# Tokens and output weights turned by transposing DMAs instead of matmuls in a BitNet attention plus quantised MLP layer

## What is computed

```
xn  = (x - mean) / sqrt(var + 1e-5)                      # per token
q, k, v = bitnet(xn, wq), bitnet(xn, wk), bitnet(xn, wv)  # 1024, 256, 256 channels
bitnet(x, w) = nan_to_num((x @ sign(w).T) * mean|w| * scale)
att = softmax(q k^T / sqrt(32)) v       # 32 heads of 32, 8 heads of keys and values
out = x + bitnet(att, wo) + (silu(xn @ G) * (xn @ U)) @ D   # G, U, D int4-like, dequantised, 3584 wide
```

## Time and profile before

| | |
|---|---|
| median of three runs | 2337.19 us |
| span of the profiled execution, first to last instruction | 2335.8 us |
| difference of the two, taken as what lies around the span | 1.4 us |
| PE busy | 2284.4 us, 98% of the span |
| DVE, ACT, POOL busy | 1809.7, 1591.0, 990.0 us |
| projections (chunks 0 to 3, `project`) | about 27 to 237 us |
| output groups (`attend_output`) | 1032.7 to 1148.6 us |

### The profile page before, as it was taken

One profiled execution on the slowest core, in us unless ns is written; L12 is line 12 of the kernel. 1 busy time (PEld: TensorE's weight loads), 2 busy tenths in 40 slices (PEclk: granted clock), 3 DMA queues, 4 the chain that ended last, 5 costly groups with the idle time before them and its releaser, 6 DMA issues.

```text
span 2335.8 us, 44834 instructions
## 1 busy us (share of the span) xinstructions
PE 2284.4 (98%) x18443; PEld 1100.0 (47%) x18443; DVE 1809.7 (77%) x2313; ACT 1591.0 (68%) x2051; POOL 990.0 (42%) x559
## 2 busy tenths in 40 slices
PE   6999999999999999999999999999999999999998
PEld 3444455555555555534444444444444444444444
DVE  8878888888888888856677777777777777777777
ACT  6774788888888888872366666666665666666664
POOL 0450699999999999960022222210002222221000
PEclk9999999999999999999999999999999999999999
DMA  5891344444444444443111111121114111114111
GB/s 187 171 202 32 70 72 78 74 76 70 72 81 72 74 72 73 80 92 136 59 37 36 44 47 37 36 109 45 37 64 145 36 36 37 38 53 181 36 36 72
DMA packets 178305, 175.51 MB, mean 75 GB/s; under 512 B 87778, under 2 KB 127586, under 8 KB 178102
## 3 DMA queue, kind: packets, MB, share of 16 engines
q1 hardware_dynamic: 113590, 143.28, 19.5%
q0 software_dynamic: 64512, 29.37, 12.6%
HBM read 160.08 MB, written 65.45 MB: 97 GB/s over the span
## 4 chain that ended last, share of the span: by engine, by line
PE 90%; DVE 5%; ACT 2%; issue 1%; DMA 1%; SPq 0%; POOL 0%; DVEq 0%; ACTq 0%
PE ps L1676 33%; PE ps L1692 17%; PE ps L1448 9%; PE ps L1501 9%; PE ps L1515 9%; PE ps L1647 5%; PE ps L1530 4%; PE ps L1473 3%; DVE sm L977 1%; DVE zone L1112 1%; DVE zone L1016 1%; ACT zone L809 0%; ACT zone L741 0%; ACT zone L789 0%; DVE zone L1388 0%
## 5 line engine op out<-in xcount | busy, mean ns | idle before, releaser
L1676 PE MATMUL ps<-xT,zone 128*128 128x512 f16 x3584 | 774.6, 379 | 2.7 <-DVE zone L1388 2.7
L1131 DVE TENSOR_REDUCE zone<-ps 128x1 f32<-128x512 f32 x1024 | 639.1, 683 | 128.1 <-PE ps L1448 120.0
L809 ACT ACTIVATE zone<-ps,sm 128x512 f32<-128x512 f32 x1024 | 628.8, 693 | 115.3 <-PE ps L1501 110.9
L649 POOL TENSOR_TENSOR zone<-zone 128x1024 f32<-128x1024 f32 x252 | 619.1, 2543 | 123.9 <-ACT zone L809 70.0
L1365 DVE TENSOR_SCALAR ps<-ps,zone_c 128x1024 f32<-128x1024 f32 x392 | 506.7, 1293 | 160.5 <-PE ps L1676 158.5
L932 ACT ACTIVATE ps<-ps,zone_c 128x1024 f32<-128x1024 f32 x392 | 426.7, 1088 | 259.9 <-PE ps L1676 259.9
L1676 PEld LDWEIGHTS ps<-xT,zone 128*128 128x128 f16 x3584 | 350.3, 98 | 426.2 <-DVE zone L1388 4.2
L1448 PE MATMUL ps<-zone 96*32 96x512 f16 (+1 forms) x3946 | 437.3, 380 | 8.6 <-issue 3.6
L1501 PE MATMUL ps<-zone 98*32 98x512 f16 x4096 | 438.3, 381 | 4.5 <-ACT zone L809 4.2
L1692 PE MATMUL ps<-zone 128*128 128x512 f16 x1792 | 387.1, 379 | 0.0
L684 POOL CAST zone<-zone 128x1024 f16<-128x1024 f32 x56 | 58.1, 1037 | 692.2 <-DVE zone L1369 692.2
(11 more groups left out here) (138 smaller groups left out, 1387.6 us busy)
## 6 DMA issues: line engine op xcount, KB each, us to landing
zone<-dequantised SPq DMA_DIRECT2D x84, 512.0 KB, 3.6
dequantised<-zero_points SPq DMA_DIRECT2D x56, 256.0 KB, 4.0
zone<-zone SPq DMA_DIRECT2D x384, 32.0 KB, 2.3
zone<-_attn_hidden_states_dram SPq DMA_DIRECT2D x16, 512.0 KB, 6.6
zone<-inverse_sums SPq DMA_DIRECT2D x128, 64.0 KB, 2.0
attention<-zone SPq DMA_DIRECT2D x32, 256.0 KB, 2.0
xT<-attention SPq DMA_DIRECT2D x4, 2048.0 KB, 12.2
dequantised<-zero_points POOLq DMA_DIRECT2D x28, 256.0 KB, 11.2
```

What stands on the lines that cost most here:

```text
L649: nc.gpsimd.tensor_tensor(duo[n % 3], prob[:, prob_slot(e), :], prob[:, prob_slot(e + 2), :], add).then_inc(s["sum_ok"], 1)
L809: A(prob[:, prob_slot(e), m % 2 * 512:(m % 2 + 1) * 512], ps[:, 3 + m % 3, :], ACT.Exp, scale=gam[:, 0:1]).then_inc(s["exp_ok"], 1)
L1131: V.tensor_reduce(mxs[:, u % 2, half, i % 16:i % 16 + 1], ps[:, (2 * i + half) % 3, :], AX, amax).then_inc(s["max_ok"], 1)
L1676: last = MM(ps[:, 4 * s2 + 2 * m + c, :], ring[:, buf, m * H + g * P:m * H + (g + 1) * P], xT[:, hf, part, g, c * 512:(c + 1) * 512], star ...
```

## The change

Chunks 1 to 3 are no longer turned by PE and no longer copied by ACT. SP issues two transposing DMAs per tile, one for the high and one for the low part, from `hst` and `lst` straight into `xT`. Chunk 0 stays on PE. The output weights are turned the same way, one DMA per tile from `wosg` into `woT`; PE's turns and DVE's copies of them go. PE, `high`, `low` and `output_signs` wait for the DMAs where they waited for PE or the copies. `low` moves one p earlier, SP's loads are interleaved with the turns, and the writes of the last quarter of `kz` wait for the last low parts.

```diff
@@ SP
+            def turn_tile(i):
+                to = slice((i % 8) * P, (i % 8 + 1) * P)
+                if i == 8:
+                    sp.wait_ge(s["z_out"], 16)
+                sp.wait_ge(s["h_ok"], i + 1)
+                sp.dma_start_transpose(xT[:, i // 8, 0, :, to], hst[:, i % 2, :]).then_inc(s[f"xh_in{i % 2}"], 16)
+                sp.wait_ge(s["l_ok"], i + 1)
+                sp.dma_start_transpose(xT[:, i // 8, 1, :, to], lst[:, i % 2, :]).then_inc(s[f"xl_in{i % 2}"], 16)
...
-            load_x(2)
-            sp.wait_ge(s["z_ok"], 1)
-            sp.dma_start(zscr.rearrange("t m c -> t (m c)"), zf16).then_inc(s["z_out"], 16)
-            load_x(3)
+            for j in range(4):
+                turn_tile(4 + j)
+                load_tile(8 + j)
+                if j == 2:
+                    sp.wait_ge(s["z_ok"], 1)
+                    sp.dma_start(zscr.rearrange("t m c -> t (m c)"), zf16).then_inc(s["z_out"], 16)
+            for j in range(4):
+                load_tile(12 + j)
+            for j in range(4):
+                turn_tile(8 + j)
...
             store_kv(0)
+            turn_tile(12)
             sp.wait_ge(s["kv_out"], 32)
             load_k(0)
+            load_q(0)
+            turn_tile(13)
             load_v(0)
-            load_q(0)
+            load_k(1)
+            turn_tile(14)
+            turn_tile(15)
             load_q(1)
             load_q(2)
-            load_k(1)
             load_m(0)
...
+            def turn_wo(i):
+                sp.wait_ge(s["wosgn_ok"], i + 1)
+                sp.dma_start_transpose(woT[:, i, :].rearrange("p (t c) -> p t c", t=KT), wosg[:, i % 2, :]).then_inc(s[f"woT_in{i % 2}"], 16)
...                                          # after the 512 steps of SP's attention loop
+            sp.wait_ge(s["snat_pe"], 1)
+            turn_wo(0)
             sp.wait_ge(s["pv_pe"], round_of(UNITS - 1, 5) + 1)
...
             load_wo(5)
+            turn_wo(1)
+            sp.wait_ge(s["pv_pe"], round_of(UNITS - 1, 7) + 1)
             for n in range(OUTPUTS):
+                if n % 2 == 1 and 2 <= (n + 3) // 2 < FQ:
+                    turn_wo((n + 3) // 2)
@@ ACT: evac_high, evac_low of tiles 4 to 15 go; high(i) for i >= 6 waits for tile i-2's DMA
+                if i >= 6:
+                    act.wait_ge(s[f"xh_in{i % 2}"], 16 * ((i - 4) // 2))
...                                          # head(2, 11)
+                if (c, f) == (2, 9):
+                    act.wait_ge(s["xl_in0"], 32 * (NC - 1))
@@ DVE: evac_output_weights goes; low(i) for i >= 6 waits for xl_in; tail(2, 11) for xl_in1
-                        elif (7 if c == 0 else 6) <= p < 10:
-                            low(i + p - 6)
+                        elif (6 if c == 0 else 5) <= p < 9:
+                            low(i + p - 5)
@@ PE: turn_high, turn_low of tiles 4 to 15 and turn_output_weights go
+                elif p == 0:
+                    for j in range(2):
+                        pe.wait_ge(s[f"xh_in{j}"], 32 * c)
+                        pe.wait_ge(s[f"xl_in{j}"], 32 * c)
...                                          # attend_output
-                    pe.wait_ge(s["woT_out"], ot + 1)
+                    pe.wait_ge(s[f"woT_in{ot % 2}"], 16 * (ot // 2 + 1))
```

More of the change, by code:

```diff
@@ L288, in layer_kernel @@
         names = """x_first0 x_first1 x_first2 x_first3 x_in1 x_in2 x_in3 w_in0 w_in1 w_in2 w_in3 w_in4 w_in5 w_in6 w_in7 par_in snat_in znat_in z_out ident sgn_done abs_done wT_pe wT_out wTv_out
-            stat_ok std_ok norm_ok xc_ok h_ok l_ok xh_pe xl_pe xh_out xl_out xlv_out snat_pe z_ok cmx_ok cmt_pe dg_ok pmr_pe pmr_ok
+            stat_ok std_ok norm_ok xc_ok h_ok l_ok xh_pe xl_pe xh_out xl_out xlv_out xh_in0 xh_in1 xl_in0 xl_in1 snat_pe z_ok cmx_ok cmt_pe dg_ok pmr_pe pmr_ok
             cm_ok cmr_ok fac_ok chain
@@ L295, in layer_kernel @@
             first0 first1 first2 first3 preset0 preset1 preset2 preset3 weights0 weights1 weights2 weights3 wgu_in0 wgu_in1 wd_in evb_ok
-            wo_in0 wo_in1 wo_in2 wo_in3 wosgn_ok woabs_ok woT_pe woT_out co_ok o_pe yo_ok ro_ok acc_ok
+            wo_in0 wo_in1 wo_in2 wo_in3 wosgn_ok woabs_ok woT_in0 woT_in1 co_ok o_pe yo_ok ro_ok acc_ok
             y_out0 y_out1 y_out2 y_out3 wr_in0 wr_in1 wr_in2 wr_in3
@@ L340, in _, with load_tile @@
         def _(sp):
+            def load_tile(i):
+                b, c, r0 = i // 8, i // 4, (i % 8) * P
+                sp.dma_start(x_tile(i), quarters(x[b, r0:r0 + P, :])).then_inc(s[f"x_in{c}" if c else f"x_first{i}"], 16)
             def load_x(c):
                 for i in range(4 * c, 4 * c + 4):
-                    b, r0 = i // 8, (i % 8) * P
-                    sp.dma_start(x_tile(i), quarters(x[b, r0:r0 + P, :])).then_inc(s[f"x_in{c}" if c else f"x_first{i}"], 16)
+                    load_tile(i)
+            def turn_tile(i):
[6 more added lines that the diff above has]
+                sp.dma_start_transpose(xT[:, i // 8, 1, :, to], lst[:, i % 2, :]).then_inc(s[f"xl_in{i % 2}"], 16)
             def load_w(k):
@@ L708, in evac_high @@
                 act.wait_ge(s["xh_pe"], i + 1)
-                if i == 8:
-                    act.wait_ge(s["z_out"], 16)
                 A(xT[:, i // 8, 0, :, (i % 8) * P:(i % 8 + 1) * P], bank16(turn_bank(i)).rearrange("p (k c) -> p k c", k=KT),
@@ L737, in high @@
                 act.wait_ge(s["xc_ok"], i + 1)
+                if i >= 6:
+                    act.wait_ge(s[f"xh_in{i % 2}"], 16 * ((i - 4) // 2))
+                elif i >= 2:
+                    act.wait_ge(s["xh_pe"], i - 1)
                 if i >= 2:
-                    act.wait_ge(s["xh_pe"], i - 1)
                     act.wait_ge(s["l_ok"], i - 1)
@@ L845, in _ @@
                         elif p == 6:
-                            evac_high(i)
                             high(i + 2)
                         elif p == 7:
-                            evac_low(i)
-                            evac_high(i + 1)
                             high(i + 3)
[L852 to L859, removed]
                 if c + 1 < NC:
@@ L882, in output_signs @@
                 if i >= 2:
-                    act.wait_ge(s["woT_pe"], i - 1)
+                    act.wait_ge(s[f"woT_in{i % 2}"], 16 * (i // 2))
                 A(wosg[:, i % 2, :], woraw[i], ACT.Sign).then_inc(s["wosgn_ok"], 1)
@@ L1023, in low @@
                 dve.wait_ge(s["h_ok"], i + 1)
-                if i >= 2:
+                if i >= 6:
+                    dve.wait_ge(s[f"xl_in{i % 2}"], 16 * ((i - 4) // 2))
+                elif i >= 2:
                     dve.wait_ge(s["xl_pe"], i - 1)
@@ L1120, in tail @@
                 dve.wait_ge(s["h2_ok"], 10 * c + p - 1)
+                if (c, f) == (2, 9):
+                    dve.wait_ge(s["xl_in1"], 32 * (NC - 1))
                 z, f0, k = (qz, b * 8 + f, 0) if f < 8 else (kz, b * 2 + (f - 8), 1)
@@ L1323, in _ @@
                         output_scales(0)
-                    elif k == 9:
-                        evac_output_weights(0)
                     if by_vector(u, 1) and k % 4 == 3:
@@ L1341, in _ @@
                 guard_attention(n)
-                if n % 2 == 0 and n // 2 + 1 < FQ:
-                    evac_output_weights(n // 2 + 1)
                 if n == 0:
@@ L1444, in row_scores @@
                     pe.wait_ge(s["max_ok"], c - 2)
+                else:
+                    pe.wait_ge(s["y_ok"], max(n for n in range(36) if output_bank(n) == c) + 1)
                 wide = P if i < LEAD else 32
@@ L1461, in project @@
                     wait_weights(pe, p)
-                if p == 0:
-                    pe.wait_ge(s["xh_out"], 4 * (c + 1))
-                    wait_low_parts(pe, 4 * (c + 1))
+                if p == 0 and c == 0:
+                    pe.wait_ge(s["xh_out"], 4)
+                    wait_low_parts(pe, 4)
+                elif p == 0:
+                    for j in range(2):
+                        pe.wait_ge(s[f"xh_in{j}"], 32 * c)
+                        pe.wait_ge(s[f"xl_in{j}"], 32 * c)
                 if n == 46:
@@ L1484, in turn_values @@
                     pe.wait_ge(s["r_ok"], 12 * c + fv + 1)
-                    if fv == 0:
-                        pe.wait_ge(s["xh_out"], 4 * (c + 1))
+                    if c:
+                        pe.wait_ge(s["v_out"], 2 * (c - 1) + fv + 1)
+                    elif fv == 0:
+                        pe.wait_ge(s["xh_out"], 4)
                     else:
-                        wait_low_parts(pe, 4 * (c + 1))
+                        wait_low_parts(pe, 4)
                     for t in range(4):
@@ L1553, in spread_maxima @@
                 last.then_inc(s["pmr_pe"], 1)
[L1555 to L1561, removed]
             turn_weights(0)
@@ L1573, in _ @@
             for c in range(NC):
-                i = 4 * (c + 1)
                 for p in range(12):
@@ L1581, in _ @@
                         turn_values(c)
[L1582 to L1590, removed]
```

(4 more changed lines are left out.)

3 lines of the change are left out of this document (removed).

## The result

The changed kernel took 2380.71 us, the median of four runs (2379.81 to 2383.14), against 2336.89 for the kernel before on the same chip: a ratio of 1.0187 with a 95% interval of 1.0175 to 1.0199, 43.8 us slower. The forecast was 2340.5, "no change"; the time is 40 us above it. The range, 2326 to 2390, holds it only because it was stretched to the packets rival's 2387: the forecast case itself ended at 2350. The profiled spans say the same, 2379.7 against 2335.8. In the profile after, the turns of tokens are L356 (high) and L358 (low), that of the output weights is L473, `project` is L1500, the first scores L1471, the output groups L1656, `high` L775, `low` L1053.

What follows compares the result with a forecast made beforehand. PE, busy 98% of the span, was taken to bound the kernel. A lead of 1.1 us after chunk 2 and +4.4 us for output weights gave +3.3, a span of 2339.1 and a median of 2340.5 us; range 2326 to 2390.

Steps and rivals of the forecast that it cites:

- packets rival: Turns priced by packets, 64 ns each: slot 4.1 us, landing 6.1, about +50 us in all, 2387; chance 0.17.
- forecast case: Transposing DMAs with a slot of 1.2 to 2.8 us, whole kernel at 2331 to 2350 us; chance 0.45.
- PE bounds the stages, and the removed turns are worth their time: In chunks 0 to 2, PE is the limit; removing 24 groups of turns at 0.44 us saves 10.6 us, plus stalls.
- (2,0): Start of the first projection of chunk 2, before at 134.0 us; claimed at 126.8 us, 7.1 us earlier.
- Chunk 0: DVE becomes the limit, PE idles 4 us, then runs a projection at low clock; the next chunk starts 2.3 us earlier.
- a slot of 2.0 us: Time until SP's queue can issue the next transposing DMA, taken between 0.32 and 4.1 us.
- a landing of 4.5 us beside POOL's DMAs: Transposing DMA's time from issue to semaphore beside POOL's DMAs; 4.0 us assumed in a quiet stretch.
- The upper ends: Highest prices considered for a transposing DMA on SP's queue: 4.1 us until the next issue, 6.1 us from issue to semaphore.
- the unlikely case: A turned part takes the 11.2 us of POOL's 256 KB DMAs; whole kernel near 2590 us; chance 0.13.
- The two buffers of `hst` don't bind: In chunk 1, `high(10)` comes 5 us after `high(8)`, whose turn has landed after 4.5 us, so no wait.
- Chunk 2: SP's loads, 10.9 us, stand between turns; the eighth part lands at 54.3 us, and chunk 3 starts at 181.1, 2.8 us earlier.
- Output weights: First tile's turn, behind SP's attention loop, idles PE 5.8 us; low clock adds 1.7, seven removed turns save 3.1: +4.4 us.

## Why the prediction failed, though its range holds the time

The hit of the range is luck: 2380.7 is 40 us above the forecast, and no case of the prediction had chunk 1 lose 32 us, chunk 2 ten and chunk 0 nothing. "No change" was also not what its own chances favoured, 0.33 against 0.42 for slower.

- **PE bounds the stages, and the removed turns are worth their time** held where the turns were hidden: (2,0) at 126.9 to 127.9 in four experiments, 126.8 forecast.
- **Chunk 0** held in mechanism: DVE's L1080 is the limit, PE idles 4.18 us (4 forecast) and (0,11) runs at the low clock. It came at 80.01 instead of 79.0: the copy moved from 80.95 to 79.27, 1.7 of the 2.6 us that I had DVE's waits give back. -1.3 instead of -2.3; where the other 0.9 went I didn't follow.
- **The failed step is the price in chunk 1**: "a slot of 2.0 us" and "a landing of 4.5 us beside POOL's DMAs". Measured 5.7 and 16.6 to 17.2. The upper ends, 4.1 and 6.1, were too low as well. The quiet prices, 1.3 and 3.2, were below what I took, so the middle of two ends was wrong on both sides: I took one price for two stages. My landing was built from quiet rows (2.0 us) while the row of the same stretch and the same size, POOL's 11.2, stood in the table and was kept for the unlikely case. The DMA share, 1.24 there and 0.00 from 70 to 72 us, was the warning.
- **"The two buffers of `hst` don't bind"** failed with it: with 17 us of landing they hold DVE for 31.3 us and ACT for 29.2, chunks 1 and 2 together.
- **Chunk 2**: the number fits by chance, 54.4 us without POOL's stream against 54.3 forecast. I had (3,0) wait for the eighth part; that part landed at 173.19 + 3.2 = 176.4, 49.5 us into the chunk, and PE waited for `load_q(0)`, ACT and DVE instead. ACT's wait in `high(15)`, which I called covered by six banks, and the stall for `load_q(0)`, which I put inside a longer one, were the path. Beside the stream chunk 2 is 60.1.
- **Output weights**: +5.0 alone, against +4.4. The wait was 4.9 us instead of 5.8, the clock 1.7 as forecast. "The later tiles have room" failed: a second wait of 1.3 us.
- **The packets rival** named 2387, near the 2380.7 measured, by terms that miss on both sides: chunk 0 at +11.2 (measured -1.3), chunk 1 at +11.4 (+32.2), chunk 2 at +20.7 (+10.2). By the packet counts its unit was right and its price wrong. It counted 1024 pieces (1056 packets measured) at 64 ns each on 16 engines, the average of the whole span, in every stretch. Quiet, they take 1.3 us instead of 4.1; beside POOL's stream the queue gets one through every 93 ns on each engine (20 us x 16 / 3429), and the slot becomes 6.2. The Trainium skill's sentence (Advanced Engine Details and Errata, X-Bar Transpose) that such DMAs are as fast as regular ones comes nearer for a quiet stretch, though the measured 1.3 and 3.2 us are above the 0.32 and 2.0 of a plain 256 KB DMA. The estimate from its VectorE page's block price, 10.5 us a part, is three times the quiet landing: the eight blocks don't add up.

## What to carry to other kernels

Before work is moved from a compute engine to DMA, read the DMA share of the very stretch it moves to: where another queue held it at 1.2, a turn landed as late as that queue's own tiles. Price a new DMA by its neighbours in that stretch and by its number of packets, not by its quiet relatives, and ask again whether its buffers cover that landing. Move only the part that falls where the share is low, here four tiles of twelve, or eight with POOL made to wait: that was 0.2% faster, the whole change 1.9% slower.

## What was not expected of the hardware

- Beside POOL's stream a transposing DMA of 128x1024 float16 goes from 1.3 to 5.7 us of issue and from 3.2 to 17 us of landing, and POOL's DMAs from 11.2 to 16.8. With 28 plain copies in POOL's place the issue stayed at 1.2 to 2.6 us, but those copies have few packets (2,240 in all, where POOL's stream has 3426 in 20 us beside the turns) and only the last of them run beside chunk 1's turns. Whether it is the number of POOL's packets or the adding that its DMAs do was not separated.
- After nearly the same idle time before (0,11), 3.9 to 4.3 us, the granted clock fell to 0.50 in seven profiles of kernels that turn tiles 4 to 7 by DMA and stayed at 1.00 in one: the 1.7 us of low clock came in most of these executions, not in all.
- The attention, the same code everywhere, took from 791 to 798 us in the profiled executions. Differences of the kernel below some five us are read from the ratios, not from one span.
